# Linear-attention layer stack on Trainium2: query exponentials rounded on GpSimd, second feed-forward product in three float32r passes, x parked in HBM

## What is computed

```python
for i in range(B):                       # B = 8 layers, H = 16 heads of K = 64
    residual = x
    Q = _feature_map(jnp.einsum('nsd,hdk->nshk', x, Wq[i]) + bq[i])   # elu(.) + 1
    Kf = _feature_map(jnp.einsum('nsd,hdk->nshk', x, Wk[i]) + bk[i])
    V = jnp.einsum('nsd,hdk->nshk', x, Wv[i]) + bv[i]
    KV = jnp.sum(Kf * V, axis=1)
    sumK = jnp.sum(Kf, axis=1)
    Z = 1.0 / (Q * sumK[:, None] + 1e-06)
    att = (Q * KV[:, None] * Z).reshape(n, s, H * K)
    y = jax.nn.gelu(att @ Wo[i] + bo[i])
    x = _layer_norm(y + residual, ln1_s[i], ln1_b[i])
    residual = x
    h = jax.nn.gelu(x @ W1[i] + b1[i])   # 128 -> 512
    h = jax.nn.gelu(h @ W2[i] + b2[i])   # 512 -> 128, the product that is changed
    x = _layer_norm(h + residual, ln2_s[i], ln2_b[i])
```

## Time and profile before

| what | us |
|---|---|
| two runs | 3315.12 and 3317.26, median 3316.19 |
| the profiled execution | 3315.69 |
| its span, first to last instruction | 3313.6 |
| stack of layers inside the span | about 840 to 3185 |

### The profile page before, as it was taken

One profiled execution on the slowest core, in us unless ns is written; L12 is line 12 of the kernel. 1 busy time (PEld: TensorE's weight loads), 2 busy tenths in 40 slices (PEclk: granted clock), 3 DMA queues, 4 the chain that ended last, 5 costly groups with the idle time before them and its releaser, 6 DMA issues. The chain is left out here.

```text
span 3313.6 us, 50990 instructions
## 1 busy us (share of the span) xinstructions
PE 2981.3 (90%) x14368; PEld 1986.3 (60%) x14368; DVE 2659.7 (80%) x10476; ACT 2443.1 (74%) x4542; POOL 855.6 (26%) x1011
## 2 busy tenths in 40 slices
PE   6999998273799999999999999999999999999758
PEld 5777776262466666665666666666666666666445
DVE  4656565853689999998999999899899999899647
ACT  5888886132588888887887887887888888888734
POOL 2444443286111111111112112111111211111136
PEclk9999998576899999999999999999999999999968
DMA  1000000323100000000000000000000000000000
GB/s 55 1 0 0 0 0 7 105 33 64 45 1 1 26 8 1 20 7 8 1 26 7 1 20 14 1 20 7 7 1 20 13 1 1 1 1 1 1 7 26
DMA packets 31561, 46.33 MB, mean 14 GB/s; under 512 B 5315, under 2 KB 21731, under 8 KB 31334
## 3 DMA queue, kind: packets, MB, share of 16 engines
q1 hardware_dynamic: 25702, 39.46, 3.6%
q0 software_dynamic: 5632, 4.20, 1.0%
HBM read 35.16 MB, written 8.49 MB: 13 GB/s over the span
## 5 line engine op out<-in xcount | busy, mean ns | idle before, releaser
L1836 DVE TENSOR_SCALAR t_feat_q<-t_recip,t_neg_mean 128x256 f32<-128x256 f32 x1024 | 399.9, 453 | 112.0 <-ACT t_recip L1701 109.4
L1549 PE MATMUL t_o_ps<-t_feat_q,t_wo 128*128 128x512 f32 x1024 | 471.9, 594 | 6.3 <-issue 3.6
L1693 ACT ACTIVATE t_recip<-t_feat_q,t_z_scale 128x256 f32<-128x256 f32 x1024 | 434.7, 499 | 1.7 <-DVE t_feat_q L1836 1.0
L1679 ACT ACTIVATE t_exp_k<-t_k_ps 128x1024 f32<-128x1024 f32 x256 | 259.7, 1014 | 231.4 <-PE t_k_ps L1526 231.4
L1799 DVE CUSTOM_DVE_ANT_0 t_junk<-t_v_ps,t_feat_k 128x256 f32<-128x256 f32 x1024 | 390.5, 419 | 7.7 <-PE t_v_ps L1526 7.3
L1948 POOL TENSOR_TENSOR t_var_eps<-t_moments,t_ln_eps 128x4 f32<-128x4 f32 x128 | 69.2, 540 | 1237.6 <-DVE t_moments L1847 1237.6
L1789 DVE SCALAR_TENSOR_TENSOR t_feat_k<-t_exp_k,t_k_ps 128x256 f32<-128x256 f32 x1024 | 369.2, 417 | 19.9 <-ACT t_exp_k L1679 19.8
L1683 ACT ACTIVATE t_exp_q<-t_q_ps 128x1024 f32<-128x1024 f32 x256 | 261.4, 1021 | 80.4 <-PE t_q_ps L1526 79.3
L1825 DVE SCALAR_TENSOR_TENSOR t_feat_q<-t_exp_q,t_q_ps 128x1024 f32<-128x1024 f32 x256 | 312.7, 1221 | 8.8
L1549 PEld LDWEIGHTS t_o_ps<-t_feat_q,t_wo 128*128 128x128 f32 x1024 | 194.1, 190 | 178.3 <-issue 158.4
L243 POOL TENSOR_TENSOR a_probs<-a_probs,a_inv 128x256 f32<-128x256 f32 (+1 forms) x256 | 208.9, 837 | 275.8 <-DVE a_inv L340 275.8
(11 more groups left out here) (373 smaller groups left out, 7522.8 us busy)
## 6 DMA issues: line engine op xcount, KB each, us to landing
t_raw_w<-in_wk SPq DMA_DIRECT2D x8, 512.0 KB, 3.8
t_raw_w<-in_wq SPq DMA_DIRECT2D x8, 512.0 KB, 4.7
t_raw_w<-in_wv SPq DMA_DIRECT2D x8, 512.0 KB, 5.6
t_raw_o<-in_wo SPq DMA_DIRECT2D x8, 512.0 KB, 3.6
t_raw<-in_w SPq DMA_DIRECT2D x16, 256.0 KB, 2.8
x<-in_x SPq DMA_DIRECT2D x4, 512.0 KB, 7.0
tokens_dram<-r_hn SPq DMA_DIRECT2D x8, 256.0 KB, 2.3
e_w_raw<-in_fc_w SPq DMA_DIRECT2D x4, 512.0 KB, 4.0
```

Of the source, the lines that this page charges most:

```text
L1549: last = pe.matmul(o_ps[:], wo[:, chunk, :], feat_q[:, s, chunk, :], start=(chunk == 0), stop=(chunk == NC - 1), skip_group_check=True)
L1679: act.activation(exp_k[:], k_ps[:], ACT.Exp, bias=-1.0).then_inc(c["k_exp"], 1)
L1693: last = act.activation(recip[:, q % 2, k * UNIT + n * SEQ:k * UNIT + (n + 1) * SEQ], feat_q[:, s, chunk, cols], ACT.Ln, bias=1.0, scale=z ...
L1836: last = dve.tensor_scalar(feat_q[:, s, chunk, cols], recip[:, q % 2, k * UNIT + n * SEQ:k * UNIT + (n + 1) * SEQ], -1.0, neg_mean[:, s, n ...
```

## The change

In the stack, four things change.

1. `feature_q`: DVE's first instruction goes. POOL does `(e + -1) + 1` on `exp_q` in place instead (`round_to_one`, two additions in one instruction, with a tiny `carry` instruction ahead that takes the wait). DVE's second instruction becomes min(max(q, 1), e), the same two operands and sizes as before.
2. `second_feed_forward`: twelve float32r matmuls instead of four float32 ones. So `hid` needs a high and a low part: ACT copies two of its four pieces at a time to `hid_hi` (`split_hid` on ACT, two 128x1024 copies a step), DVE subtracts (`split_hid` on DVE, two 128x1024 subtractions a step). `swap_w2` on POOL makes the low part of the weights too.
3. `x` is stored to HBM at the end of `combine_and_entry_phase` (eight DMAs of 256 KB), its place in SBUF serves as `raw_o`, `raw_1`, `raw_2` and `hid`, and it is read back in two 1 MB loads, one late in the stack and one first in SP's list of `finish_phase`, ahead of that phase's weights.
4. POOL's list of a step gets four `round_to_one`, so its weight swaps of step t mod 8 = 2 come behind the fourth.

The core of the diff:

```diff
             def second_feed_forward(u, follows):
-                pe.wait_ge(c["hid_ready"], 4 * u + 5)
+                pe.wait_ge(c["hid_hi_ready"], 2 * u + 3)
+                pe.wait_ge(c["hid_split"], 2 * u + 2)
                 pe.wait_ge(c["w2_ready"], layer_of(u) + 2)
                 if follows:
                     pe.wait_ge(c["state_t_ready"], u - 1 + 2 + PER)
                 for j in range(NF):
-                    last = pe.matmul(m0[:], w2[:, j, :], hid[:, j, :], start=(j == 0), stop=(j == NF - 1))
+                    pe.matmul(m0[:], w2_hi[:, j, :], hid_hi[:, j, :], start=(j == 0), stop=False, skip_group_check=True)
+                    pe.matmul(m0[:], w2_lo[:, j, :], hid_hi[:, j, :], start=False, stop=False, skip_group_check=True)
+                for j in range(NF):
+                    if j == 2:
+                        pe.wait_ge(c["hid_split"], 2 * u + 3)
+                    last = pe.matmul(m0[:], w2_hi[:, j, :], hid_lo[:, j, :], start=False, stop=(j == NF - 1), skip_group_check=True)
                 last.then_inc(c["w2_filled"], 1)
...
+            def split_hid(u, h):
+                act.wait_ge(c["hid_ready"], 4 * u + 2 * h + 3)
...
+                act.activation(hid_hi[:, 2 * h:2 * h + 2, :], hid[:, 2 * h:2 * h + 2, :], ACT.Copy).then_inc(c["hid_hi_ready"], 1)
...
                     exp_queries(t, 1)
                 if Dn:
+                    split_hid(t - 3, 0)
                     first_gelu(t - 3, 2)
                     first_gelu(t - 3, 3)
...
                 if A:
                     exp_queries(t, 2)
+                if Dn:
+                    split_hid(t - 3, 1)
                 if E:
                     act.wait_ge(c["n2_turned"], t - 4 + 2)
...
             def feature_q(t, s, q):
-                dve.wait_ge(c["q_exp"], 4 * t + q + 2)
-                dve.tensor_scalar(exp_q[:], exp_q[:], 1.0, -1.0, ALU.min, ALU.add).then_inc(c["q_less_one"], 1)
-                dve.wait_ge(c["q_less_one"], 4 * t + q + 2)
-                dve.scalar_tensor_tensor(feat_q[:, s, 2 * q:2 * q + 2, :], exp_q[:].rearrange("p (k t) -> p k t", k=2), 1.0,
-                                         q_ps[:].rearrange("p (k t) -> p k t", k=2), ALU.add, ALU.max).then_inc(c["q_ready"], 1)
+                dve.wait_ge(c["q_rounded"], 4 * t + q + 2)
+                dve.scalar_tensor_tensor(feat_q[:, s, 2 * q:2 * q + 2, :], q_ps[:].rearrange("p (k t) -> p k t", k=2), 1.0,
+                                         exp_q[:].rearrange("p (k t) -> p k t", k=2), ALU.max, ALU.min).then_inc(c["q_ready"], 1)
...
+            def split_hid(u, h):
+                dve.wait_ge(c["hid_hi_ready"], 2 * u + h + 2)
+                dve.tensor_tensor(hid_lo[:, 2 * h:2 * h + 2, :], hid[:, 2 * h:2 * h + 2, :],
+                                  hid_hi[:, 2 * h:2 * h + 2, :].bitcast(F32), ALU.subtract).then_inc(c["hid_split"], 1)
...
                     feature_q(t, s, 1)
+                if Dn:
+                    split_hid(t - 3, 0)
...
                     layernorm_stats(t - 2, 0, m1, c["z1_turned"], c["bn1_done"], c["stats1_ready"])
+                if Dn:
+                    split_hid(t - 3, 1)
                 if A:
                     feature_q(t, s, 2)
...
+            def round_to_one(t, q):
+                pool.wait_ge(c["q_exp"], 4 * t + q + 2)
+                carry(3)
+                pool.tensor_scalar(exp_q[:], exp_q[:], -1.0, 1.0, ALU.add, ALU.add).then_inc(c["q_rounded"], 1)
...
+                if A:
+                    round_to_one(t, 2)
                 if C:
                     rstd_of(t - 2, 0, c["stats1_ready"], c["var1_ready"], c["rstd1_ready"])
-                if active(at, 0) and at != UNITS - 1:
+                if A and at != UNITS - 1:
                     split_x(t + 1, r)
+                if A:
+                    round_to_one(t, 3)
...
         @block.sync
         def _(sp):
+            sp.dma_start(g["x"][:, 16:32, :], g["x_dram"][:, 16:32, :]).then_inc(c["x_in"], 16)
             sp.dma_start(w_raw[:], d["w_mix"]).then_inc(c["w_in"], 16)
```

More of the change, by code:

```diff
@@ L1195, in first_layer_tiles @@
     g["t_bv_all"] = sb("t_bv_all", [P, LAYERS, NC])
-    names = ("k_filled k_exp k_ready q_filled q_exp q_less_one q_ready v_filled v_drained kv_step scale_ready kv_ready "
+    names = ("k_filled k_exp k_ready q_filled q_exp q_rounded q_ready v_filled v_drained kv_step scale_ready kv_ready "
              "ln_ready recip_ready att_ready o_filled y1_ready z1_ready z1_turned bn1_done stats1_ready var1_ready rstd1_ready "
[1 row of a table removed]
[1 row of a table added]
              "bn2_done stats2_ready var2_ready rstd2_ready n2_ready n2_turned state_t_ready x_hi_ready x_split "
[1 row of a table removed]
-             "raw_w_in raw_b_in raw_o_in raw_1_in raw_2_in").split()
[1 row of a table added]
+             "raw_w_in raw_b_in raw_o_in raw_1_in raw_2_in x_in").split()
     g["t_sems"] = {n: sem("t_" + n) for n in names}
@@ L1227, in combine_and_entry_phase @@
         names = ("ones_made zeroed diag_ready gate_filled term_ready x_added bn_done stats_ready var_ready rstd_ready xn_ready "
-                 "x_turned state_ready w_in b_in const_in hi_ready lo_ready bias_ready").split()
+                 "x_turned state_ready x_stored w_in b_in const_in hi_ready lo_ready bias_ready").split()
         c = {n: sem("n_" + n) for n in names}
@@ L1246, in _ @@
             sp.dma_start(g["t_bv_all"][:], d["bv"]).then_inc(c["const_in"], 16)
+            for n in range(TURNS):
+                sp.wait_ge(c["x_added"], n + 1)
+                sp.dma_start(g["x_dram"][:, GT * n:GT * n + GT, :], g["x"][:, GT * n:GT * n + GT, :]).then_inc(c["x_stored"], 16)
             t = g["t_sems"]
@@ L1394, in stack_phase @@
         w1_lo = sb("t_w1_lo", [P, FF], F32R)
-        w2 = sb("t_w2", [P, NF, D])
+        w2_hi = sb("t_w2_hi", [P, NF, D], F32R)
+        w2_lo = sb("t_w2_lo", [P, NF, D], F32R)
         x_hi = sb("t_x_hi", [P, 2, UNIT], F32R)
@@ L1416, in stack_phase @@
         x1_lo = sb("t_x1_lo", [P, UNIT], F32R)
-        hid = sb("t_hid", [P, NF, UNIT])
+        hid = g["x"][:, 16:32, :].rearrange("p (j a) d -> p j (a d)", j=NF)
+        hid_hi = sb("t_hid_hi", [P, NF, UNIT], F32R)
+        hid_lo = sb("t_hid_lo", [P, NF, UNIT], F32R)
         y2 = sb("t_y2", [P, UNIT])
@@ L1506, in _ @@
                 load_rest(n + 1)
+            sp.wait_ge(c["wo_ready"], LAYERS + 1)
+            sp.wait_ge(c["w1_ready"], LAYERS + 1)
+            sp.wait_ge(c["w2_ready"], LAYERS + 1)
+            sp.dma_start(g["x"][:, 0:16, :], g["x_dram"][:, 0:16, :]).then_inc(c["x_in"], 16)
+            sp.wait_ge(c["x_in"], 17)
         @block.tensor
@@ L1669, in first_gelu @@
                 act.wait_ge(c["w1_filled"], 4 * u + j + 2)
+                if j == 0:
+                    act.wait_ge(c["hid_split"], 2 * u + 1)
                 act.activation(hid[:, j, :], (m1, m0)[j % 2][:], ACT.Gelu_apprx_tanh, bias=param(u, 1 + j)).then_inc(c["hid_ready"], 1)
+            def split_hid(u, h):
+                act.wait_ge(c["hid_ready"], 4 * u + 2 * h + 3)
+                if h == 0 and (not isinstance(u, int) or u >= 1):
+                    act.wait_ge(c["w2_filled"], u + 1)
+                act.activation(hid_hi[:, 2 * h:2 * h + 2, :], hid[:, 2 * h:2 * h + 2, :], ACT.Copy).then_inc(c["hid_hi_ready"], 1)
             def split_weights(layer, w, k):
@@ L1931, in swap_wo @@
                 carry(0)
-                copy(wo[:], raw_o[:]).then_inc(c["wo_ready"], 1)
+                copy(wo[:], raw_o).then_inc(c["wo_ready"], 1)
             def swap_w1(layer):
@@ L1936, in swap_w1 @@
                 carry(1)
-                copy(w1_hi[:], raw_1[:]).then_inc(c["w1_hi_ready"], 1)
+                copy(w1_hi[:], raw_1).then_inc(c["w1_hi_ready"], 1)
                 pool.wait_ge(c["w1_hi_ready"], layer + 2)
-                pool.tensor_tensor(w1_lo[:], raw_1[:], w1_hi[:].bitcast(F32), ALU.subtract).then_inc(c["w1_ready"], 1)
+                pool.tensor_tensor(w1_lo[:], raw_1, w1_hi[:].bitcast(F32), ALU.subtract).then_inc(c["w1_ready"], 1)
             def swap_w2(layer):
@@ L1943, in swap_w2 @@
                 carry(2)
-                copy(w2[:], raw_2[:]).then_inc(c["w2_ready"], 1)
+                copy(w2_hi[:], raw_2).then_inc(c["w2_hi_ready"], 1)
+                pool.wait_ge(c["w2_hi_ready"], layer + 2)
+                pool.tensor_tensor(w2_lo[:], raw_2, w2_hi[:].bitcast(F32), ALU.subtract).then_inc(c["w2_ready"], 1)
             def rstd_of(u, j, stats_ready, var_ready, rstd_ready):
@@ L1959, in step @@
                 s, r = at % 2, 1 - at % 2
-                C, Dn, E = (active(at, k) for k in (2, 3, 4))
+                A, C, Dn, E = (active(at, k) for k in (0, 2, 3, 4))
                 if at == 0:
@@ L2050, in finish_phase @@
         out_ps = [ps(f"f_out_ps{i}", [P, 2, 4, D]) for i in range(2)] + [turned]
-        names = ("w_in gate_in b_in b_zeroed made order_made b_step b_ready w_hi_ready w_split diag_ready gate_filled gate_copied "
```

(3 more changed lines are left out.)

18 lines of the change are left out of this document (12 added, 6 removed), and 4 rows, old and new, of the table names.

## The result

The changed kernel takes 3842.91 us (2 runs, 3842.51 to 3843.3) against 3316.19: ratio 1.1585, 95% interval 1.156 to 1.161. The forecast was 3381 with a range of 3355 to 3420, so the time lies far above the range. The profiled execution spans 3841.3 us.

What follows compares the result with a forecast made beforehand. PE looked like the bound, with ACT equally tight ahead of E's turn. 1.11 us per step over 60 steps (+66.6), with the edges +65.0, on 3315.7 plus 0.5 gave 3381 us, range 3355 to 3420.

Steps and rivals of the forecast that it cites:

- The rounding on POOL: Behind each query exponential: POOL's chain takes 1.28 us, 1.05 of it the instruction; DVE loses 0.70, four times a step.
- quarter 3: Fourth query quarter of a step: rounding not hidden by other DVE work, 0.70 goes and 1.28 comes, +0.58 per step.
- One sign: If the forecast is right, PE idles about 0.3 us ahead of `biases` 3, waiting on key features.
- the body: The 60 steps from the fourth to the last but one: 0.53 plus 0.58, 1.11 us per step, +66.6.
- the edges: Outside ordinary steps: weight swaps -5.4 us in seven layers, first three steps +1.7, last four nothing, finish +2.1.
- The split on ACT and DVE: Two ACT copies of 0.96 us and two DVE subtractions of 1.14 a step; query features start 1.40 later.
- one tight place: ACT ahead of the last two gelus: the first copy delays the turn of E's rows by 0.96 us.
- The product in three passes: Second feed-forward product on PE: twelve passes 0.23 us apart take 2.76; 0.78 saved from product to bias.
- PE's gain is used up waiting: `biases` 3 on PE waits for the keys read, so it comes 0.53 us later despite 0.78 saved.
- the first rival: E's turn not held by the gelu, nothing moves by 0.96: +0.15 us per step, 3324 us; chance 0.12.
- The third: Three passes save nothing: passes 0.40 us apart, 2.80 more per step with the rounding, 3482 us; chance 0.03.
- The second: POOL's rounding and DVE's second subtraction block each other: 0.55 us per step, 33 more, 3414 us; chance 0.12.

Runs made afterwards that it cites:

- quick pairs: Kernel before plus 24, then 18 one-input POOL instructions behind the layers' last step: multiply-add, add-multiply, multiply twice 1.05 us; minimum-maximum 1.04.
- the copy's form: Changed kernel with POOL's rounding instruction as times 1.0 plus 0.0, in place on the same buffer: 3400.99 us, ratio 1.0247.
- the split alone: Changed kernel with the rounding put back on DVE as before; hid's split, three passes and x in HBM stay: 3404.48 us, ratio 1.0264.
- the two quick instructions: Changed kernel with POOL's rounding as two instructions, times 1.0 minus 1.0, then times 1.0 plus 1.0: 3617.84 us, ratio 1.0906.

## Why the prediction was wrong, step by step

**The rounding on POOL: the failed step.** "I take 1.05, the one-input copy of 128x1024 with two operations on constants, because size, input count and form are the same." The form was not the same: the copy multiplies and adds, the change adds twice, and that took 3.64. The upper bound, 2.58 from a two-input instruction, was no bound either: a one-input instruction can cost more than a two-input one of its size. The rest of the chain was right: with 1.05 in its place the time from the exponential to the rounding's end was 1.285 us for the 1.28 forecast. By the Trainium skill (GPSIMD Engine Reference, 4.1 Engine selection) one-input element-wise work on GpSimd is roughly at line rate. The quick pairs agree with it, 1.05 us for 1024 columns; the two additions with 3.64 and the single ones with 2.8 do not, and the measurement decides.

**What followed from it.** The forecast had the rounding show in quarter 3 alone, +0.58, and quarters 0 to 2 covered. With 3.87 in place of 1.28 for the chain, quarter 3 takes 3.15 more, all that was added. Quarter 2 takes 1.21 more, where with the copy's form it takes 0.48 less: its cover had ended already with 2.57. Quarter 1 gives way by 0.42. Quarter 0 takes 2.30 more, most of it TensorE's clock by an estimate from the rows in the last section. 442 us of the 527 are this one price and what it brings with it.

**The rest of the sum.** With the copy's form the kernel took 3401, 20 over the forecast and inside its range, and there the terms can be read one by one. PE's timeline of an ordinary step (t = 32) in that kernel, to lay beside the earlier trace rows:

```profile
2009.52 0.39 PE L1531 MATMUL t_k_ps<-t_ones_b,t_b 3*128 3x512 bf16 x2 [0.90 <-DVE t_feat_q L1853]
...
2034.72 0.50 PE L1585 MATMUL t_m<-t_hid_hi,t_w_hi 128*128 128x512 f32 x1 [0.32 <-ACT state_t L1781]
...
2038.56 0.39 PE L1531 MATMUL t_k_ps<-t_ones_b,t_b 3*128 3x512 bf16 x2
...
2045.70 0.39 PE L1531 MATMUL t_k_ps<-t_ones_b,t_b 3*128 3x512 bf16 x2 [0.90 <-DVE t_feat_q L1853]
```

Counted from the first bias, the product starts 0.93 later than before (forecast 0.96), `biases` 3 comes 0.45 later (0.53) and the next step 1.00 later (1.11); PE's idle time ahead of `biases` 0 is the forecast 0.9. So with the right price the mechanism holds, not only the number. One sign is missing: in this step PE does not wait the forecast 0.3 ahead of `biases` 3.

Starts of the steps against those of before, in that run: the 42 ordinary steps take 1.03 more each, forecast 1.11. The 12 steps around the weight swaps take 11.6 more in all (forecast 7.1: 12 x 1.11, seven times -1.17, five times 0.4), the six at the loop's ends 17.2 (7.5, by the same terms), the first three 7.4 (1.7), the last four with the finish 7.8 (2.1). So the body was right, and the edges, taken at little or nothing, made the 20 us. What the loop's ends wait for was not settled.

**The split on ACT and DVE.** The sum was right; its reading as one tight place was not. "The first falls into the time in which DVE waits for the later turn" is true, but the reverse holds too, at least with VectorE's own rounding in place: without the later turn the subtractions are late by as much or more (1.43 in quarter 2 instead of 0.26). Moving the copy alone gains nothing.

**The product in three passes.** The pace was right: passes start 0.23 to 0.24 apart. "PE's gain is used up waiting" was too strong. The forecast's own sum kept 0.43 of its gain of 0.78 (0.96 less 0.53), and the timeline above keeps 0.48 (product to bias 3.84 us for 4.32). The full gain shows only where both preparations are off the path: 3.65 us, so 0.67.

**Rivals.** The turn is held by the gelu: the first rival fell, PE's wait names it. The third fell with the pace of the passes. The second, the blocking of POOL and DVE, was not what made the time: with the copy's form no subtraction started over 0.4 us ahead of a rounding's end. With the two additions DVE's subtraction beside POOL was not stretched at all (group mean 1206, as in the split alone); with the two quick instructions it was:

```profile
L1871 DVE TENSOR_TENSOR t_hid_lo<-x,t_hid_hi 128x1024 fp32r<-128x1024 f32 x128 | 188.1, 1470 | 9.2 <-ACT t_hid_hi L1697 9.2
```

By the Trainium skill (SBUF — State Buffer, "Who interferes with whom") a DVE instruction with two SBUF inputs and a GpSimd one that reads SBUF exclude each other. The quick pairs agree; the two additions read SBUF as well and the trace shows no such stretch: of 61 subtractions that started at least 0.4 us ahead of the end of one, the median was 1192 ns, of the others 1216.

## What to carry to other kernels

Take an instruction's price from a row with the same operations, not only the same engine, size and input count; where none exists, measure the exact form before building on it, for here it decided 442 of 527 us. A bound from "a heavier instruction" holds only if heavier is known to be slower on that engine. Where two engines' new work hides under each other's wait, undoing one alone can show nothing (the copy) or less than half (the subtractions): undo both. And where a total comes out as forecast, look at its parts before believing the reason.
